# Another order for the first tiles of a Mamba-2 mixer: ScalarE's decays, exponentials, SiLU and table copies, GpSimd's weight splits, VectorE's first mask

## The reference, cut to what matters

```python
proj = hidden_states @ in_proj_w.T                       # hidden (2, 512, 512)
gate, xBC, dt = jnp.split(proj, [INTER, INTER + CONV_DIM], axis=-1)
xBC = silu(causal_conv_of_4_taps(xBC) + conv_b)          # a depthwise convolution
x, Bm, Cm = jnp.split(xBC, [INTER, INTER + NG * SS], axis=-1)
dt = jnp.clip(jax.nn.softplus(dt + dt_bias), 0.001, 100.0)
cs = jnp.cumsum(dt * A, axis=-1)                         # in chunks of 128 tokens
Lmat = jnp.where(tri, jnp.exp(cs[..., :, None] - cs[..., None, :]), 0.0)
Ydiag = ((C @ B.T) * Lmat) @ (x * dt)
states = B.T @ (exp(cs[..., -1:] - cs) * x * dt)         # carried from chunk to chunk
Yoff = exp(cs) * (C @ previous_states)
yg = (Ydiag + Yoff + x * D) * silu(gate)
out = rms_norm_in_groups(yg) * norm_w @ out_proj_w.T     # groups of 1024 channels
```

## Time and profile before

| | us |
|---|---|
| median of three runs | 2412.69 |
| the three runs | 2409.28 to 2413.34 |
| the profiled execution | 2411.45 |
| its span, first to last instruction | 2409.7 |
| TensorE busy in it | 2345.8 |
| VectorE, ScalarE, GpSimd busy | 1793.7, 1577.7, 1243.6 |
| mean granted TensorE clock | 0.994 |

### The profile page before, as it was taken

How to read it: one execution, slowest core, us unless ns; L and a number is a source line. 1 busy time by engine, 2 the same in 40 slices (tenths; PEclk the granted TensorE clock), 3 DMA queues, 4 the chain that set the end, 5 groups by cost and what they waited for, 6 DMA issues and landing times.

```text
span 2409.7 us, 48597 instructions
## 1 busy us (share of the span) xinstructions
PE 2345.8 (97%) x15424; PEld 1365.4 (57%) x15624; DVE 1793.7 (74%) x3230; ACT 1577.7 (65%) x3324; POOL 1243.6 (52%) x1001
## 2 busy tenths in 40 slices
PE   7999999999999999999999999889999999999998
PEld 4555555555555555555555555455656556556544
DVE  6777787777777777777777778677777777888714
ACT  7676776767777777776776767366565656665533
POOL 4555456556456456556555548644444444445223
PEclk9999999999999999999999999999999999999999
DMA  7343343343343343344333334021100110111000
GB/s 262 112 134 108 110 129 110 105 138 112 112 125 113 110 129 120 108 123 127 105 125 121 118 122 135 1 90 44 45 20 26 45 46 1 45 71 36 13 1 36
DMA packets 113894, 218.83 MB, mean 91 GB/s; under 512 B 9696, under 2 KB 43104, under 8 KB 111424
## 3 DMA queue, kind: packets, MB, share of 16 engines
q1 hardware_dynamic: 113600, 215.28, 27.6%
HBM read 212.10 MB, written 3.15 MB: 89 GB/s over the span
## 4 chain that ended last, share of the span: by engine, by line
PE 89%; DVE 3%; ACT 3%; POOL 2%; issue 1%; DMA 1%; SPq 0%; ACTq 0%; DVEq 0%; POOLq 0%
PE bank L60 23%; PE bank L61 22%; PE bank L59 21%; PE bank L808 5%; PE bank L820 3%; PE bank L812 3%; PE bank L1822 3%; PE bank L829 2%; PE bank L2250 1%; PE bank L2260 1%; PE bank L2251 1%; PE bank L2259 1%; PE bank L2273 1%; ACT ecs L1907 1%; PE bank L2271 1%
## 5 line engine op out<-in xcount | busy, mean ns | idle before, releaser
L282 DVE SCALAR_TENSOR_TENSOR xc<-bank,taps,xc 128x511 f32<-128x511 f32 (+2 forms) x384 | 284.7, 741 | 40.6 <-ACT xc L269 23.4
L1026 ACT ACTIVATE E<-wq,cst 128x128 f32<-128x128 f32 x1024 | 311.8, 389 | 1.3 <-DMA wq<-cs_rows 1.3
L1389 POOL TENSOR_TENSOR xw<-xt,wdec 128x384 f32<-128x384 f32 x128 | 106.4, 832 | 327.5 <-ACT xc L274 166.2
L1398 POOL TENSOR_TENSOR acc<-acc,sq 128x512 f32<-128x512 f32 x112 | 163.2, 1457 | 185.1 <-ACT sq L1038 185.1
L59 PE MATMUL bank<-xhi,wx 128*128 128x512 f16 x640 | 244.2, 382 | 0.5 <-DVE xc L282 0.5
L61 PE MATMUL bank<-xhi,wx 128*128 128x512 f16 x640 | 242.8, 379 | 0.0
L60 PE MATMUL bank<-xlo,wx 128*128 128x512 f16 x640 | 242.8, 379 | 0.0
L1189 DVE TENSOR_TENSOR E<-E,cbm 128x1024 f32<-128x1024 f32 x128 | 239.1, 1868 | 4.7 <-ACT E L1032 4.7
L1384 POOL TENSOR_TENSOR ecs<-ecs,xcC 128x768 f32<-128x768 f32 x128 | 239.9, 1874 | 0.0
L1038 ACT ACTIVATE sq<-u 128x512 f32<-128x512 f32 x112 | 70.5, 630 | 253.5 <-DVE u L1270 253.5
L1265 DVE SCALAR_TENSOR_TENSOR u<-xc,D,bank 128x512 f32<-128x512 f32 x128 | 95.5, 746 | 158.5 <-PE bank L812 149.3
(11 more groups left out here) (300 smaller groups left out, 6233.7 us busy)
## 6 DMA issues: line engine op xcount, KB each, us to landing
wq<-cs_rows SPq DMA_DIRECT2D x128, 512.0 KB, 4.0
ecs<-ecs_rows SPq DMA_DIRECT2D x128, 384.0 KB, 3.6
wx<-in_w_xbc SPq DMA_DIRECT2D x80, 256.0 KB, 2.7
wz<-in_w_z SPq DMA_DIRECT2D x64, 256.0 KB, 2.6
wo<-in_w_o SPq DMA_DIRECT2D x64, 256.0 KB, 4.2
wq<-in_wq SPq DMA_DIRECT2D x8, 1024.0 KB, 5.8
awo<-in_wo SPq DMA_DIRECT2D x8, 1024.0 KB, 4.9
wkv<-in_wkv SPq DMA_DIRECT2D x8, 512.0 KB, 4.0
```

What stands on the lines that cost most here:

```text
L282: self.nc.vector.scalar_tensor_tensor(out=dst[:, d:T], in0=self.k.bank[bank][:, 0:T - d], scalar=self.taps[:, bass.ds(g, 1), b, j, 3 - d:4 ...
L1026: ins = nc.scalar.activation(E[t.i % 4][:, h, c], sc.csr[t.i % 2][:, h, c * P:(c + 1) * P], ACT.Relu, scale=-1.0, bias=head(sc.cst, t, c, h))
L1398: nc.gpsimd.tensor_tensor(acc[t.b][:], acc[t.b][:], sq[:], ALU.add).then_inc(acc_done, 1)
```

## The change

On ScalarE, decays(0) goes ahead of silu 3, tap 4 and turned_B. exps(1) comes out of slot 0 to the place right behind decays(1). decays(2) and exps(2) come behind gate(1) in slot 0, one on each side of silu of tile 3, and decays(3) goes behind exps(2) to the end of the slot. evacuate 6 and 7 go behind silu 4. On GpSimd, the split of gate weight 2 goes into first(), ahead of decayed_x(1); those of weights 3 and 4 go ahead of decayed_x(2) in slot 0, with the split of x weight 7 between them. On VectorE, scale_norm (with a semaphore of its own, nw_ok) goes ahead of conv 1, and the first masked_CB ahead of turned_x(0). No work is added or left out.

```diff
@@ ScalarE
                 gate(tile_at(0, 0))
+                decays(tile_at(0, 0))
                 sc.silu(act, 3, su.conv_out(3))
                 su.tap(act, 4)
                 turned_B(tile_at(0, 0), ring_bank(1, USE_BT))
-                decays(tile_at(0, 0))
                 exps(tile_at(0, 0))
                 decays(tile_at(0, 1))
+                exps(tile_at(0, 1))
                 su.decay_rows(act, 1)
                 su.decays_to_ends(act, 1)
                 su.evacuate(act, 4)
                 su.evacuate(act, 5)
-                decays(tile_at(0, 2))
 
             def slot(g, m):
                 s = tile_at(g, m)
-                if m % 2 == 0:
+                if m % 2 == 0 and not is_first(s):
                     for d in (1, 2):
                         if tile_at(g, m + d):
                             exps(tile_at(g, m + d))
                 if is_first(s):
-                    su.evacuate(act, 6)
-                    su.evacuate(act, 7)
-                    act.wait_ge(su.v, 13)
+                    act.wait_ge(su.nw_ok, 1)
                     act.wait_ge(su.taps_in, 16)
                 square(s)
                 leading(s)
                 if is_first(s):
                     sc.silu(act, 4, su.conv_out(4))
+                    su.evacuate(act, 6)
+                    su.evacuate(act, 7)
@@
-                    decays(t)
+                    if not is_first(s):
+                        decays(t)
                 if tile_at(g, m + 1):
                     gate(tile_at(g, m + 1))
+                if is_first(s):
+                    decays(tile_at(0, 2))
                 if t:
                     sc.silu(act, q, sc.xc[t.i % 4])
+                if is_first(s):
+                    exps(tile_at(0, 2))
+                    decays(t)
@@ VectorE
                 su.ahead_of_exp(dve, 1)
+                su.scale_norm(dve)
                 su.conv(dve, 1)
@@
                 dve.wait_ge(su.ev, 2)
+                masked_CB(tile_at(0, 0), ring_bank(1, USE_CB))
                 turned_x(tile_at(0, 0))
-                su.scale_norm(dve)
-                masked_CB(tile_at(0, 0), ring_bank(1, USE_CB))
                 su.conv(dve, 4)
@@ GpSimd
                 sc.split_wx(pool, 0, 6)
+                sc.split_wz(pool, 0, 2)
                 decayed_x(tile_at(0, 1))
@@
+                if is_first(s):
+                    sc.split_wz(pool, 0, 3)
+                    sc.split_wx(pool, 0, 7)
+                    sc.split_wz(pool, 0, 4)
                 if tile_at(g, m + 2):
                     decayed_x(tile_at(g, m + 2))
                 if is_first(s):
-                    sc.split_wx(pool, 0, 7)
-                    for j in range(2, XT):
+                    for j in range(5, XT):
                         sc.split_wz(pool, 0, j)
```

More of the change, by code:

```diff
@@ L314, in __init__ @@
         self.a, self.v, self.g = S("su_act"), S("su_dve"), S("su_pool")
-        self.tr, self.ev, self.consts = S("su_tr"), S("su_ev"), S("su_consts")
+        self.tr, self.ev, self.consts, self.nw_ok = S("su_tr"), S("su_ev"), S("su_consts"), S("su_nw")
         self.cs_out, self.ecs_out = S("su_cs_out"), S("su_ecs_out")
@@ L477, in scale_norm @@
         dve.wait_ge(self.rest_in, 16 * 3)
-        self.nc.vector.tensor_scalar(self.sc.nw[:], self.sc.nw[:], SPREAD, None, ALU.mult).then_inc(self.v, 1)
+        self.nc.vector.tensor_scalar(self.sc.nw[:], self.sc.nw[:], SPREAD, None, ALU.mult).then_inc(self.nw_ok, 1)
     def remainder1(self, pool, kt):
```

## The result

The changed kernel takes 2432.41 us (median of six runs, 2428.93 to 2437.26), the kernel before 2411.25 us beside it: a ratio of 1.009, 95% interval 1.0079 to 1.0101. It is **slower by about 21 us**, or 0.9%. Slower was forecast, but by 7.7 us, with 2422.5 as the upper end of the range. The mechanism named (a table load in the loop's body) is there; its size was less than half of what it is.

The account below looks back on a forecast made before the run. TensorE, busy 97% of the time, was taken to bound the kernel. Start +0.6 us and loop +7.1 us gave +7.7: 2419.2 from the profiled execution, 2420.4 from the median, middle 2419.8 us; range 2411.5 to 2422.5.

Parts of the forecast that it names:

- What bounds the kernel: Whole kernel: TensorE is busy 97% of the time; in the loop's odd slots ScalarE is only just ahead of it.
- The spare of 1.4 us: Slots 17 to 97: ScalarE's gate is ahead of TensorE's need by 0.01 to 0.42 us each, 1.4 us in sum.
- The price of the load: Between decays and gate: 3.75 us with a table load, 2.34 us without, so 1.41 us a load.
- Part 1: Start up to scan(1): ScalarE work leaves the stretch where TensorE waits; scan(1) at 55.3 instead of 61.77, 6.5 us sooner.
- The edits costed at nothing: Start, on GpSimd and VectorE: earlier weight splits, scale_norm and masked_CB cost or gain nothing.
- Part 2: Up to scan(3): late wo(1) and a table load leave 1.7 us at scan(2); the clock makes scan(3) +0.6 us.
- The two moved prices: Ahead of scan(2): TensorE waits some 5 us there, and its low-clock price of 2.3 us moves from slot 1 to slot 2.
- Part 3: Loop body: gate's table load also runs in six later rounds, +7.1 us; one ahead of square would cost nothing.
- The sum: Whole kernel: 0.6 us at the start and 7.1 us in the loop make +7.7 us.
- A load put right once ahead of the loop: Rival, between slots 0 and 1: six later rounds pay no table load; +0.6 us, 2412.7 us; chance 0.16.
- The drain rival: Rival, at table loads: each also empties ScalarE's pipe, 2.66 us a switch with 1.38 of drain; 2427 us; chance 0.02.

Follow-up runs that it names:

- r4: Changed kernel plus an explicit load of Exp's table as first instruction of slot 1 in the loop's body: 2421.77 us, ratio 1.0041.
- r1: Changed kernel plus one explicit load of SiLU's table at the end of slot 0, behind decays(3): 2411.24 us, ratio 0.9998.
- r5: Changed kernel plus SiLU's table loaded at the end of slot 0, and SyncE's load of wo(1) ahead of its wait for decays(3): 2407.14 us, ratio 0.9987.
- r7: Changed kernel with exps(2) ahead of silu of tile 3 in slot 0, no explicit table load: 2410.96 us, ratio 1.0.
- r3: Changed kernel plus an explicit load of SiLU's table as first instruction of slot 1 in the loop's body: 2411.10 us, ratio 1.0.
- r8: Kernel before with only decays(0) moved ahead of silu 3 and exps(1) behind decays(1): 2408.78 us, ratio 0.9992.
- r6: Kernel before with only the GpSimd and VectorE parts of the change: 2408.88 us, ratio 0.9996.

## Why the prediction was wrong, point by point

**What bounds the kernel.** Right. The loop is TensorE's, and the odd slots have no room for ScalarE. The spare of 1.4 us that I added up from single rows of the six slots, 0.24 us a slot, was not there when it was needed: r4 lost 1.44 us a slot for a load priced at 1.41. The price of the load held (3.75 us from decays to gate in r4, 2.34 before). But VectorE's product, which releases square, ended 5.17 us after the start of its scan in r4 on average over the six slots, and 4.94 before, and those 0.23 us are the spare. In single slots of all these kernels it ends 4.25 to 5.58 us after it. A distance read in one execution was taken as a reserve; the sum should have kept it as an end of the range.

**Part 1.** scan(1) was forecast at 55.3 and came at 55.68, its gate at 54.94 for 54.6. Counted from the store of cs the gain is smaller and scatters: 3.5 us in the changed kernel, 5.2 in r1, 6.5 in r5, against the 6.5 forecast. Counted from scan(0) it takes two values: 5.2 us in the changed kernel, r1, r4 and r7, and 7.1 in r3 and r5. ScalarE's own work was priced right, 5.23 us from square(0) to gate(1) for 5.25. What differs is VectorE's product that square(0) waits for, and GpSimd's decayed_C(1) beside it. First the changed kernel, then r3:

```profile
47.58 2.01 DVE L1276 TENSOR_TENSOR u<-u,gz 128x512 f32<-128x512 f32 x1
...
47.22 1.82 POOL L1390 TENSOR_TENSOR ecs<-ecs,xcC 128x768 f32<-128x768 f32 x1
```

```profile
47.55 0.68 DVE L1278 TENSOR_TENSOR u<-u,gz 128x512 f32<-128x512 f32 x1
...
47.76 2.15 POOL L1392 TENSOR_TENSOR ecs<-ecs,xcC 128x768 f32<-128x768 f32 x1
```

Before, decayed_C(1) started at 49.79, behind the product; counted from scan(0), the new order lets GpSimd come to it 1.7 us sooner. In the five executions where GpSimd starts first (the changed kernel, r1, r4, r7, r8) VectorE's product takes 1.54 to 2.01 us and ends 0.54 to 0.55 us behind GpSimd's instruction; in the other five it takes 0.68 to 0.71. The forecast had no term for this. That scan(1) still came within 0.4 us of it was partly luck: the delay was offset by a scan(0) that came 0.85 us sooner in that execution. The edits costed at nothing show no effect by themselves (r6).

**Part 2.** Right in every link, somewhat short in size. ScalarE's wait for wo(1), and scan(2) behind it, in the changed kernel:

```profile
68.21 0.62 ACT L255 COPY wohi<-wo 128x512 bf16<-128x512 bf16 x1 [2.25 <-DMA wo<-in_w_o]
...
71.86 1.28 ACT L1045 ACT_TABLE_LOAD   x1
...
73.89 1.12 PE L808 MATMUL bank<-E,xt 128*64 128x128 f32 x8 [5.80 <-ACT gz L1045]
```

lead_wo(1) was forecast at 67.5, scan(2) at 73.2 after a wait of some 5 us. The two moved prices are there: scan(2) runs at 1.2 GHz (the clock was 0.56 from 74 to 80 us), and slot 2 took 15.79 us, 2.4 more than before, for 2.3 forecast. Scan(3) came 1.4 us late for 0.6, 2.3 us late if counted from scan(0), and 4.0 if counted from the store of cs. r5 shows that the queue behind decays(3) was what took the gain back: without it 3.1 to 3.9 us are left at the end.

**Part 3, the step that failed.** The forecast saw both loads, and gave the one ahead of square the price nothing, because "it falls into ScalarE's wait for VectorE's product there". No row of before showed a load at an instruction that waits for VectorE. The one load of before next to a wait, the first of the program, did stand ahead of it; the wait was for a DMA:

```profile
0.73 1.28 ACT L400 ACT_TABLE_LOAD   x1 [0.73 <-PEq L2499]
4.59 0.62 ACT L400 CAST xhi<-wohi 128x512 f16<-128x512 f32 x1 [2.57 <-DMA wohi<-in_hidT]
```

In the loop's body it stands behind: 5.2 to 5.7 us of waiting precede each of the six later loads at L1038. Why the two places differ, no run tests. The true price of the load ahead of square is 8.6 us (after less r4), as high as that of gate's load (8.6, r4 less before, for 7.1). Together 17.2 us in the six slots instead of 7.1. r3 puts a load on the other side of the wait, and it is free.

**The sum.** 1.4 us at scan(3) and 17.2 in the six slots, less 0.5 in all other slots, make 18.1 us at scan 127 in the profiled executions; the spans differ by 19.7 and the medians by 21.2. Of the remaining 3.1 us, 1.7 lie behind scan 127, a stretch that takes 890.0 to 892.5 us in the ten profiled executions with no edit in it. The other 1.4 is the distance of the two profiled executions from their medians (2431.16 for 2432.41, and 2411.45 for 2411.25).

**The rivals.** A load put right once ahead of the loop didn't come true. The drain rival is out: 3.74 us from decays to gate with a load leaves no room for the 1.38 us that the Trainium skill, ScalarE: Activation LUTs, section "What ACT_TABLE_LOAD costs", adds to each switch. The rule of the Trainium skill, ScalarE: Activation LUTs, section "Table sets: the hidden batching unit", to batch by set, points the right way, but r3 bounds it: seven more loads in the right place cost nothing.

## What to carry to other kernels

A loop's body should be entered with the same function table that it leaves with. If a moved exponential changes the table at the entry, the body gets loads that run in every round, and one explicit load ahead of the loop, or one swap of two lines, removes them. Look in the rows on which side of a wait a table load stands: behind a wait for another engine it is added to the path in full. And when work is moved off the way of one wait, read what the queues hold behind the moved instruction; here a weight load behind decays(3) took back most of 6 us.

## What the runs showed of the hardware that I had not expected

ScalarE's first instruction of a round comes late even when it waits for no one. The loads at the head of the body in r3 and r4 have idle time before them that the trace puts down to "issue", which means that nothing in the profile was waited for. In slot 17 it is 3.49 us in r3 and 3.42 in r4; over the six later rounds it is 2.13 to 3.49 us in r3 and 3.33 to 3.89 in r4. The load of the first round, which ScalarE reaches from slot 0 without turning back, has none. That left only 0.52 us of a wait of 5.3 us over behind the load of slot 17 in r3, and in r4:

```profile
255.70 1.28 ACT L1088 ACT_TABLE_LOAD   x1 [3.42 <-issue]
257.74 0.63 ACT L1038 ACTIVATE sq<-u 128x512 f32<-128x512 f32 x1 [0.75 <-DVE u L1278]
```

Idle time at the head of a loop's body is thus not all free: of some 5.4 us, 2.1 to 3.9 go to the turn of the loop itself. That it is the turn is read from the first round's load, and no run tests it further.
